# First adapter layer: the totals of the query weights one place later, their followers one step later

## The reference

```python
def _L0_ffn_ref(x, W_base, b_base, W_gate, A, B):
    result = jnp.einsum('bnd,od->bno', x, W_base) + b_base
    probs = jax.nn.softmax(jnp.einsum('bnd,ed->bne', x, W_gate), axis=-1)
    top_p, top_i = jax.lax.top_k(probs, TOP_K)
    ...
    hw = jnp.einsum('bnd,erd->bner', x, A) * route_w[..., None]
    return result + jnp.einsum('bner,eor->bno', hw, B) * SCALING
...
x = x + _L0_ffn_ref(_layernorm(x, axis=-1), ...)
```

## Time and profile before

| | |
|---|---|
| three runs, median (lowest to highest) | 1673.65 us (1672.67 to 1675.62) |
| the profiled execution's own time | 1664.38 us |
| its span, first to last instruction | 1662.6 us |
| TensorE busy | 1566.5 us, 94% |
| DVE busy | 1034.3 us, 62% |
| ACT busy | 873.2 us, 53% |
| POOL busy | 811.3 us, 49% |
| mean granted clock of TensorE | 0.984 |

### The profile page before, as it was taken

How to read it: one execution, slowest core, us unless ns; L and a number is a source line. 1 busy time by engine, 2 the same in 40 slices (tenths; PEclk the granted TensorE clock), 3 DMA queues, 4 the chain that set the end, 5 groups by cost and what they waited for, 6 DMA issues and landing times. The chain is left out here.

```text
span 1662.6 us, 32076 instructions
## 1 busy us (share of the span) xinstructions
PE 1566.5 (94%) x12430; PEld 960.8 (58%) x12430; DVE 1034.3 (62%) x2764; ACT 873.2 (53%) x1670; POOL 811.3 (49%) x699
## 2 busy tenths in 40 slices
PE   6997799999877999999999999979999999999998
PEld 5665355555443777777677777644444444465554
DVE  6897757766777888888888888833111010254433
ACT  6687222221656999999999999942110000111110
POOL 4222344444763888888888888840010000144440
PEclk9899899999999999999999999999999999999999
DMA  9696434544553999999999998997963431123331
GB/s 333 221 330 206 88 74 117 152 140 125 103 115 80 174 175 191 182 182 176 223 187 175 195 176 170 183 180 196 233 171 80 102 89 26 63 55 92 82 93 65
DMA packets 559752, 249.32 MB, mean 150 GB/s; under 512 B 502256, under 2 KB 535152, under 8 KB 559216
## 3 DMA queue, kind: packets, MB, share of 16 engines
q1 hardware_dynamic: 559600, 247.26, 64.6%
HBM read 73.15 MB, written 48.23 MB: 73 GB/s over the span
## 5 line engine op out<-in xcount | busy, mean ns | idle before, releaser
L1884 POOL TENSOR_TENSOR xb<-xb 128x1280 f16<-128x1280 f32 x128 | 335.7, 2622 | 8.4 <-ACT xb L1770 8.4
L1762 ACT ACTIVATE xb<-so,D_sv,qw_c 128x512 f32<-128x512 f32 (+3 forms) x512 | 289.2, 623 | 3.2 <-DVE D_sv L1827 3.1
L1818 DVE TENSOR_REDUCE so<-so 128x1 f32<-128x512 f32 (+3 forms) x512 | 227.9, 491 | 19.9 <-PE so L1714 19.2
L1770 ACT ACTIVATE xb<-xb 128x1280 f16<-128x1280 f32 x128 | 162.6, 1271 | 14.0 <-DMA xb<-xb 10.1
L92 POOL TENSOR_SCALAR mv<-mv 128x1 f32<-128x1 f32 x64 | 31.2, 488 | 282.1 <-DVE mv L87 281.0
L2009 DVE SCALAR_TENSOR_TENSOR xb<-so,ms_c,xb 128x512 f32<-128x512 f32 x32 | 22.5, 746 | 228.0 <-PE so L50 228.0
L1705 PE MATMUL so<-kTh,D_QTh 128*128 128x512 f16 (+3 forms) x512 | 153.6, 300 | 7.6 <-ACT xb L1762 7.5
L1706 PE MATMUL so<-kTl,D_QTh 128*128 128x512 f16 (+3 forms) x512 | 153.3, 299 | 0.0
L1707 PE MATMUL so<-kTh,D_QTl 128*128 128x512 f16 (+3 forms) x512 | 146.7, 299 | 0.0
L1729 PE MATMUL D_t<-vh,xb 128*128 128x65 f16 x1280 | 131.5, 194 | 6.3 <-DVE D_on L1837 4.2
L1890 POOL TENSOR_TENSOR D_qs<-D_qs,D_t 128x256 f32<-128x256 f32 x128 | 92.9, 726 | 89.5 <-DVE D_t L1851 89.5
(11 more groups left out here) (306 smaller groups left out, 4221.9 us busy)
## 6 DMA issues: line engine op xcount, KB each, us to landing
A_wo<-in_wo SPq DMA_DIRECT2D x16, 1024.0 KB, 6.3
od<-D_os SPq DMA_DIRECT2D x32, 512.0 KB, 4.5
mwd<-A_mst SPq DMA_DIRECT2D x32, 256.0 KB, 3.1
xd<-xb SPq DMA_DIRECT2D x16, 512.0 KB, 4.1
ow_raw<-mwd SPq DMA_DIRECT2D x16, 512.0 KB, 4.9
xb<-xd SPq DMA_DIRECT2D x16, 512.0 KB, 5.9
out_x<-xb SPq DMA_DIRECT2D x16, 512.0 KB, 3.5
xb<-in_x SPq DMA_DIRECT2D x6, 1024.0 KB, 14.5
```

The lines of the kernel that those rows point to most:

```text
L1762: m = e.activation(p[:, AT[i]:AT[i] + N], Sb[n % 4][:, c:c + N], ACT.Exp, scale=qw.col(qw.NEG, g), bias=s[:, 7 - i:8 - i])
L1770: e.activation(P2[u % 3][:, 0:1280], P[u % 3][:, :], ACT.Copy).then_inc(s_ph, 1)
L1818: m = e.tensor_reduce(minima(u, i), Sb[n % 4][:, c:c + N], AX.X, ALU.min)
L1884: e.tensor_tensor(P2[u % 3][:, 1280:2560], P[u % 3][:, :], P2[u % 3][:, 0:1280], ALU.subtract).then_inc(s_pl, 1)
```

## The change

The totals stand one place later in ORDER: not behind the adapter product of their tile but behind the first column block of the next. What needs them follows a step later or later in the step: the DVE reads a total after the next gate, `dve_inverses` and `dve_low` move from before `finish` to behind `adapter` in the same step, POOL's scale stands at the end of the next step, the inverses of the smaller weights stand in step 5, and a group's store is issued a step later. The loads of the raw weights keep their place on SP and their wait.

```diff
     for t in range(2, NT):
-        ORDER += [("c", t, 0), ("c", t, 1), ("w", t), ("c", t, 2), ("a", t)]
-        if t == WA:
+        ORDER += [("c", t, 0)]
+        if t == WA + 1:
             ORDER += [("s", 4), ("s", MS)]
-        if QW <= t < QW + 8:
-            ORDER += [("s", 5 + t - QW)]
+        if QW < t <= QW + 8:
+            ORDER += [("s", 4 + t - QW)]
+        ORDER += [("c", t, 1), ("w", t), ("c", t, 2), ("a", t)]
...
-            if t == WA + 1:
+            if t == WA + 2:
                 wa.dve_inverses(e, w)
                 ms.dve_inverse(e, w)
...
+            if t == WA + 1:
+                total(4)
+                total(MS)
+            if QW < t <= QW + 8:
+                total(4 + t - QW)
             low_w(t)
+            finish(t)
+            adapter(t)
             if QW < t <= QW + 8:
                 qw.dve_inverses(e, w, t - QW - 1)
                 qw.dve_low(e, w, t - QW - 1)
-            finish(t)
-            adapter(t)
-            if t == WA:
-                total(4)
-                total(MS)
-            if QW <= t < QW + 8:
-                total(5 + t - QW)
...
-            if t == WA:
+            if t == WA + 1:
                 scale(4)
                 scale(MS)
-            if QW <= t < QW + 8:
-                scale(5 + t - QW)
+            if QW < t <= QW + 8:
+                scale(4 + t - QW)
...
-            if QW < t <= QW + 8:
-                qw.sp_store(e, w, t - QW - 1)
+            if QW + 1 < t <= QW + 9:
+                qw.sp_store(e, w, t - QW - 2)
             if QW - 1 <= t < QW + 7:
                 lw.all_split(w)
                 qw.sp_load(e, w, t - QW + 1)
```

## The result

The changed kernel takes 1689.55 us, the kernel before 1673.38 us: a ratio of 1.0098, 95% interval 1.0071 to 1.0125. It is slower by 16 us, where 13 were forecast; the interval is 12 to 21 us.

What follows compares the result with a forecast made beforehand. TensorE was taken as busiest, the DVE close to being the bound; 9.8 us from loads and tile pace plus 3.3 us of clock gave 13.1 us, 1673.65 to 1686.8 us, range 1677 to 1694.

Steps and rivals of the forecast that it cites:

- The totals' wait goes: On TensorE, totals moved behind the next tile's first columns lose their 8.6 us wait; about 10 us if nothing else is late.
- Tiles 3 to 5 even out: Gate 4 gains 1.57 us, given back by gate 5 through totals and inverses; gate 6 stays at 270.4.
- The load behind dve_low, weigh behind the load, the gate behind weigh: Gates 6 to 12: raw-weight load waits for the later dve_low, the DVE stands still 2.1 us; 16.63 us a tile, 12.0 lost.
- The term of 9.8 us: Total delay at the turn of tile 14, 399.4 against 389.53, before the clock's price; TensorE carries it through.
- TensorE's clock: After longer waits at the turn of the weights, the granted clock falls: 0 to 1.7 us per tile, 3.3 us in all.
- 1.1 us in three of six tiles: The clock's price as taken, the DVE hiding some of it: 3.3 us.
- clock in every tile: Rival: the clock falls after every wait and the DVE hides nothing; 20 us slower, 1693.7 us; chance 0.10.
- Tiles 12 and 13 go at TensorE's pace: These tiles have dve_low but no load, so TensorE sets the pace: turns 13.18 + 0.26, then 13.18 us apart.
- All gained: Rival: nothing takes the place of the removed wait; 10 us faster, 1663.7 us; chance 0.05.
- Load hidden: Rival: the raw-weight load does not hold up weigh; each tile takes 14.5 us, 1670.7 us; chance 0.04.
- Quick load: Rival: the load lands in 2.4 us, with no fall of the clock; 2.6 us slower, 1676.2 us; chance 0.08.

Runs made afterwards that it cites:

- the run with the bias ahead: Run with weigh behind low_w, plus POOL's bias taken one tile ahead and weigh between finish's second and third parts: ratio 0.9938, 1656.81 us against 1667.48.
- the third buffer: Changed kernel with three buffers of raw query weights in place of two: ratio 0.9983, 1665.82 us against 1667.82 for the kernel before.
- the filled runs: Changed kernel with sixteen unread matmuls ahead of the turns of tiles 7 to 12, run twice: 1680.52 and 1678.84 us, ratios 1.0061 and 1.0039.
- the run with weigh later: Changed kernel with the DVE's weigh moved from before the gate to behind low_w: ratio to the kernel before 0.9962, on another chip 0.9983.
- the bias beside the gate: Changed kernel with weigh behind low_w and POOL's bias ahead of the low half of the activations: ratio 1.0153 to the kernel before, 1697.42 us.

## Why the prediction was right, point by point

- **The totals' wait goes, and that is some 10 us.** Borne out as far as shown. It came only once the DVE had room: 10.1 us by the turns in the run with the bias ahead, whose other two edits no run has without the new order.
- **Tiles 3 to 5 even out.** Right to 0.05 us: with the 10.83 us of the earlier start taken off, turns 5 and 6 stand at 259.0 and 272.9, as gates 256.44 and 270.4 and the 2.55 us from gate to turn had it.
- **The load behind dve_low, weigh behind the load, the gate behind weigh.** Right, and settled by the third buffer. Tile 9: next gate after 16.55 us, 16.63 forecast. Weigh waits for its DMA in just the six tiles named, though in the first two of them only 0.8 us, because the split of the smaller weights fills part of the time. In the filled runs a tile took 16.3 to 16.4 us, and the second load landed after 3.3 us in place of the 3.6 taken. The term of 9.8 us was 7.9 and 8.6 by the turns there, and 12.7 and 6.4 by the medians of two chips. In the changed kernel itself, where the loads landed later, it was 19.5 - 8.3 = 11.2 us and 16.1 - 4.7 = 11.4 by the turns.
- **TensorE's clock.** The direction was right, the size was not: 3.3 us were forecast, 8.3 and 4.7 measured in the two executions of the changed kernel. The step that failed is "1.1 us in three of six tiles", and in it the number of tiles. The clock fell behind five and four of the six turns, after waits of 2.1 us and more; the length of the wait alone does not decide, for behind 3.24 us in tile 9 it stayed at 1.00. The price of 1.1 us held: in tiles 7 to 11 the way from the gate to the end of dve_low, 10.9 us at the full clock, took 0.8 to 1.2 us more in six of seven falls, so the DVE hid a part as forecast, and 2.4 in tile 10, where the clock was 0.50 and then 0.70. In tile 12, with TensorE setting the pace behind it, a fall cost 2.5 and 1.7 us. The priced rival "clock in every tile", 20 us, almost meets the 19.5 us of the profiled execution, but by luck: 3.2 of these are later loads, and the DVE hid a part.
- **Tiles 12 and 13 go at TensorE's pace.** Nearly: 419.84 - 390.76 = 29.1 us for 26.6, the first of them again at the lower clock.
- **Rivals.** All gained: not without moving more. Load hidden: 2.9 us less than before was its price, and the third buffer, which makes it so, measured 2.0 by the medians (the interval takes in no change) and 1.4 by the turns. Quick load: no second load landed in under 3.2 us.
- Open is why loads landed late. That of tile 11 took 5.3 us where the others that weigh waited for took 3.2 to 4.3, and kept weigh waiting for 3.81 us; in the second execution of the changed kernel it took 5.0, in the filled runs 3.3 and 3.4. The three latest (4.3, 5.3, 5.0) each had a transfer of the queue q8, which the profile calls instruction, beside them; but so had two that came in time (3.3 here, 3.6 before), and with the third buffer a load took 5.5 us without one. It is a hint at most and was not tried.

## What to carry to other kernels

A step that is moved "later" drags along everything that waits for its end: look at the wait that the diff does not show, here a buffer that comes free at the end of a tile and whose reload stands at the start of the next. A wait removed on the busiest engine is worth its length only if the next engine's chain is shorter than the pace that would follow; add that chain up before counting the gain. And when a wait on TensorE grows from about 1 to over 2 us, price its clock too: here it fell behind four or five of six such waits, at about 1.1 us each where the DVE hid a part and about 2 where it did not. Last, an edit that fills a wait can move other things as well: compare the other waits before the whole gain is put down to one cause.

## What the runs showed of the hardware that was not expected

DVE instructions of very different sizes can last until the GpSimd instruction beside them ends: 1.74 us for one column of 128 numbers, 2.17 for eight, 2.44 for a 0.41 us multiplication, each ending within 0.2 us of POOL's. The reciprocal just ahead of the first, also beside POOL's bias, kept its 0.16 us. The Trainium skill, "SBUF — State Buffer", section "Who interferes with whom", says that the two engines share one pair of ports, held for a whole instruction by whoever issues first, which DVE instructions with two inputs there and some forms of `tensor_scalar` need; the rows agree, and they show that the price is what is left of POOL's instruction, whatever the DVE's length. It also bears on which order on POOL is good: with the bias beside the gate turns 3 to 14 were 28.6 us longer than in the run with weigh later (181.2 against 152.6), falls of the clock included (0.57 behind the turn of tile 11); with the bias one tile ahead and weigh inside finish they were 4.1 us shorter (148.5).
